# Scores taken relative to key 0 of each head, and key 0's score made from the row maximum, in a cross-attention kernel

## What is computed

```python
def xattn(q, latent_kv, Wq, Wkv_expand, Wout):   # q: 8 x 1024 x 1024, latent_kv: 8 x 64 x 256
    qp = q @ Wq.T
    k, v = split(latent_kv @ Wkv_expand.T, 2)    # 64 keys a batch, 16 heads of 64
    scores = einsum('bhqd,bhkd->bhqk', qh, kh) / sqrt(64)
    scores = where(tril(ones(1024, 64)), scores, finfo.min)
    attn = softmax(scores)
    return (attn @ vh) @ Wout.T

x = x + xattn(layernorm(x), ctx_512, Wq, Wkv_expand, Wout)
x = x + ffn(layernorm(x), weight)                # one fp8-quantised 1024 x 1024 linear layer
```

## Time and profile before

| | us |
|---|---|
| median of 3 runs | 1786.26 (1785.97 to 1786.73) |
| the profiled execution | 1787.1 |
| its span, from first to last instruction | 1785.3 |
| TensorE busy in the span | 1730.4 |
| VectorE busy | 1327.3 |
| ScalarE busy | 688.7 |
| mean granted TensorE clock | 0.988 |

### The profile page before, as it was taken

How to read it: one execution, slowest core, us unless ns; L and a number is a source line. 1 busy time by engine, 2 the same in 40 slices (tenths; PEclk the granted TensorE clock), 3 DMA queues, 4 the chain that set the end, 5 groups by cost and what they waited for, 6 DMA issues and landing times.

```text
span 1785.3 us, 25886 instructions
## 1 busy us (share of the span) xinstructions
PE 1730.4 (97%) x10457; PEld 827.7 (46%) x10482; DVE 1327.3 (74%) x1813; ACT 688.7 (39%) x643; POOL 185.4 (10%) x143
## 2 busy tenths in 40 slices
PE   8689999999999999999999999999999999799998
PEld 4434454445444544454445444544454444344444
DVE  6776778677866787778787878787878665777775
ACT  6632133223322332233223322332233221599996
POOL 0000000000000000000000000000000002155555
PEclk9799999999999999999999999999999999899999
DMA  9674555544555445554555445544553444799995
GB/s 318 155 193 119 126 116 117 131 123 119 111 138 124 110 113 133 133 109 108 132 137 114 107 127 129 129 106 120 136 124 98 119 118 101 250 318 319 319 318 181
DMA packets 404429, 272.15 MB, mean 152 GB/s; under 512 B 355056, under 2 KB 357616, under 8 KB 403824
## 3 DMA queue, kind: packets, MB, share of 16 engines
q1 hardware_dynamic: 404336, 270.84, 57.3%
HBM read 119.28 MB, written 71.30 MB: 107 GB/s over the span
## 4 chain that ended last, share of the span: by engine, by line
PE 91%; issue 5%; DVE 2%; ACT 1%; DMA 1%; POOL 0%; SPq 0%; POOLq 0%; DVEq 0%; ACTq 0%
PE ps_all L636 71%; PE ps_all L772 12%; PE ps_all L623 2%; PE ps_all L609 1%; PE ps_all L610 1%; PE ps_all L645 1%; PE ps_all L706 1%; PE ps_all L588 1%; DVE n_buf L1093 1%; ACT tile_space L869 0%; ACT n_buf L857 0%; DMA tile_space<-tile_space 0%; DVE amax L1072 0%; DMA tile_space<-in_ctx_dram 0%; PE ps_all L578 0%
## 5 line engine op out<-in xcount | busy, mean ns | idle before, releaser
L636 PE MATMUL ps_all<-m_buf,tile_space 128*128 128x512 f16 x3072 | 681.0, 381 | 4.8 <-DVE wo_t L1294 4.8
L636 PE MATMUL ps_all<-n_buf,tile_space 128*128 128x512 f16 x3024 | 670.1, 379 | 0.0
L636 PEld LDWEIGHTS ps_all<-m_buf,tile_space 128*128 128x128 f16 x3072 | 298.0, 98 | 368.8 <-issue 12.2
L636 PEld LDWEIGHTS ps_all<-n_buf,tile_space 128*128 128x128 f16 x3024 | 291.6, 98 | 350.6 <-issue 6.2
L883 ACT ACTIVATE tile_space<-tile_space,neg_mean 128x1024 f32<-128x1024 f32 x63 | 72.4, 1150 | 327.7 <-DVE neg_mean L1180 327.7
L527 POOL TENSOR_TENSOR rstd_x<-veps_x,minus_half 128x1 f32<-128x1 f32 x64 | 35.3, 551 | 1388.4 <-DVE veps_x L1123 1388.4
L879 ACT ACTIVATE tile_space<-tile_space,score_scale 128x1024 f32<-128x1024 f32 x64 | 73.4, 1147 | 230.6 <-DVE tile_space L1150 230.6
L875 ACT ACTIVATE tile_space<-tile_space 128x1024 f16<-128x1024 f32 x64 | 67.6, 1057 | 184.4 <-DVE tile_space L1160 184.4
L1110 DVE SCALAR_TENSOR_TENSOR tile_space<-tile_space 128x1024 f16<-128x1024 f32 x64 | 78.4, 1225 | 64.0 <-ACT tile_space L875 64.0
L772 PE MATMUL ps_all<-wo_t,tile_space 128*128 128x512 bf16 x512 | 119.9, 383 | 2.4 <-DVE tile_space L1401 1.2
L1154 DVE TENSOR_REDUCE hsum<-tile_space 128x16 f32<-128x1024 f32 x64 | 77.9, 1217 | 59.5 <-ACT tile_space L879 59.5
(11 more groups left out here) (131 smaller groups left out, 1700.7 us busy)
## 6 DMA issues: line engine op xcount, KB each, us to landing
tile_space<-in_x_dram SPq DMA_DIRECT2D x128, 512.0 KB, 3.9
x_scratch<-tile_space SPq DMA_DIRECT2D x64, 512.0 KB, 3.0
m_buf<-x_scratch SPq DMA_DIRECT2D x32, 512.0 KB, 5.6
tile_space<-x_scratch SPq DMA_DIRECT2D x32, 512.0 KB, 5.8
out_dram<-m_buf SPq DMA_DIRECT2D x32, 512.0 KB, 4.5
out_dram<-tile_space SPq DMA_DIRECT2D x31, 512.0 KB, 5.0
m_buf<-in_L_xattn_Wq_dram SPq DMA_DIRECT2D x4, 1024.0 KB, 11.1
n_buf<-in_L_xattn_Wout_dram SPq DMA_DIRECT2D x2, 2048.0 KB, 18.3
```

The lines of the kernel that those rows point to most:

```text
L636: mm = nc.tensor.matmul(to[:, cols], left[:, ls, c * P:(c + 1) * P], right[:, rs, c, cols], start=(c == 0 and i == 0), stop=(c == CT - 1 a ...
```

## The change

The scores of each head are taken relative to the score of the head's key 0, which leaves the softmax as it is. So keys are made from the context minus its batch's row 0 (`ctx_d`, one VectorE subtraction during setup, on which TensorE's first `expand` waits), and the column of key 0, which would be zero, is left out of M. M has 63 columns a head: 8 x 63 = 504 of them, contiguous, for each half of the score product. Its `take_m` read 1008 of the 1024 PSUM columns. The score matmuls stream 504 columns, the second half starting 504 columns (1008 bytes) into the block. `make_m` still makes all 64 columns.

Key 0's score in the softmax is made from the maximum of the 63: the row maximum is max(hmax, 0), so key 0's entry is min(-hmax, 0), and this same number is added to the other 63. That is one more small VectorE instruction, with a wait before and after. The maximum and the addition read 2 x 8 x 63 columns. The mask is added in two instructions, one a bank.

```diff
--- before.py
+++ after.py
@@ -64,6 +64,8 @@
     T = B * TB
     KEYS = B * SK
     HALF = 512
+    REST = SK - 1
+    RH = NH // 2 * REST
     assert SK == HD and NP == CT and KEYS == HALF and TB == 8
 
     x_rows = x.rearrange("b s h -> (b s) h")
@@ -162,7 +164,7 @@
         wkv_f = tile_space[:, 8:12, :].rearrange("p a (b l) -> p (a b) l", l=L)
         ctx_f = tile_space[:, 12, :].rearrange("p (a l) -> p a l", l=L)
         wkv_t = tile_space[:, 4:8, :].rearrange("p (a q) r -> p a (q r)", a=LT)
-        ctx_t = tile_space[:, 3, :].rearrange("p (a k) -> p a k", a=LT)
+        ctx_t, ctx_d = (tile_space[:, i, :].rearrange("p (a k) -> p a k", a=LT) for i in (3, 2))
         k_f = wo_t[:, 1].rearrange("p j c -> p (j c)").bitcast(F32).rearrange("p (j k) -> p j k", k=KEYS)
         v_f = w8_raw[:].rearrange("p j c -> p (j c)").bitcast(F32).rearrange("p (j k) -> p j k", k=KEYS)
         k_hi_t, k_lo_t = (tile_space[:, i:i + 2, :].rearrange("p a c -> p (a c)").bitcast(F16)
@@ -185,6 +187,8 @@
         got_wout = [sem(f"got_wout{i}") for i in range(2)]
         turned = sem("turned")
         turned_read = sem("turned_read")
+        ctx_made = sem("ctx_made")
+        key0_made = sem("key0_made")
         wt_full = sem("wt_full")
         wt_hi = sem("wt_hi")
         wt_free = sem("wt_free")
@@ -327,6 +331,18 @@
         KEYS_AT_S = {3: 0, 6: 1}
         KEYS_AT_O = {1: (2,), 2: (3,), 4: (4,), 6: (5,), 7: (6,), 8: (7,)}
 
+        def rest_of(to):
+            return to.rearrange("p (h k) -> p h k", k=SK)[:, :, 1:SK]
+
+        def keys_of(s, c):
+            return m_buf[:, s, c, 0:NH * REST].rearrange("p (h k) -> p h k", k=REST)
+
+        def by_bank(t):
+            return t.rearrange("p (b n) -> p b n", b=2)
+
+        rest_scores = by_bank(ps_s)[:, :, 0:RH].rearrange("p b (h k) -> p b h k", k=REST)
+        sub_heads = sub.rearrange("p (b h k) -> p b h k", b=2, k=SK)
+
         block = scope.enter_context(nc.Block())
 
 
@@ -581,12 +597,15 @@
 
             def expand(g2):
 
+                if g2 == 0:
+                    pe.wait_ge(ctx_made, 1)
+                of = ctx_d if g2 < QUAD else ctx_t
                 to = next_slot()
                 for half in range(2):
                     g = 2 * g2 + half
                     for lt in range(LT):
                         mm = nc.tensor.matmul(to[:, half * HALF:(half + 1) * HALF],
-                                              wkv_t[:, lt, g * P:(g + 1) * P], ctx_t[:, lt, :],
+                                              wkv_t[:, lt, g * P:(g + 1) * P], of[:, lt, :],
                                               start=(lt == 0), stop=(lt == LT - 1))
                 mm.then_inc(turned, 1)
 
@@ -626,6 +645,20 @@
                                 if i == len(PASSES) - 1 and half == 1 and q == 1:
                                     mm.then_inc(grow_full[k], 1)
 
+
+            def scores(left, weave=lambda c: None, ready=lambda c: None):
+                for c in range(CT):
+                    ready(c)
+                    for i, (ls, rs) in enumerate(PASSES):
+                        for half in range(2):
+                            mm = nc.tensor.matmul(ps_s[:, half * HALF:half * HALF + RH],
+                                                  left[:, ls, c * P:(c + 1) * P],
+                                                  m_buf[:, rs, c, half * RH:(half + 1) * RH],
+                                                  start=(c == 0 and i == 0),
+                                                  stop=(c == CT - 1 and i == len(PASSES) - 1))
+                    if c == CT - 1:
+                        mm.then_inc(s_full, 1)
+                    weave(c + 1)
 
             def split_product(to, left, right, full, weave=lambda c: None, ready=lambda c: None):
                 for c in range(CT):
@@ -684,7 +717,7 @@
                             pe.wait_ge(grow_free[c % 2], uses(b + 1, 0, c) + 1)
 
                     between(0)
-                    split_product(ps_s, xt_buf[1 - e], m_buf, s_full, between, m_chunk)
+                    scores(xt_buf[1 - e], between, m_chunk)
                 if last and 1 <= tt <= 4:
                     turn_w8(tt - 1)
                 if b == 2 and is_step(tt, 5):
@@ -746,7 +779,7 @@
             for k in range(2):
                 pe.wait_ge(grow_free[k], QUAD)
             pe.wait_ge(x_turned, 16)
-            split_product(ps_s, xt_buf[0], m_buf, s_full)
+            scores(xt_buf[0])
 
             for b in range(B):
                 batch(pe, b, step, unroll=(b == B - 1))
@@ -859,7 +892,7 @@
 
             def take_m(c, n):
                 act.wait_ge(grow_full[c % 2], n + 1)
-                nc.scalar.activation(m_buf[:, 0, c, :], grow_ps[c % 2][:], ACT.Copy,
+                nc.scalar.activation(keys_of(0, c), rest_of(grow_ps[c % 2][:]), ACT.Copy,
                                      scale=M_SCALE).then_inc(grow_hi[c % 2], 1)
 
             def x_high(t, e):
@@ -1051,6 +1084,11 @@
                 dve.wait_ge(scales_made, n)
 
 
+            dve.wait_ge(turned_read, 1)
+            by_batch = lambda t: t.rearrange("p a (b k) -> p (a b) k", k=SK)
+            nc.vector.tensor_tensor(by_batch(ctx_d), by_batch(ctx_t),
+                                    by_batch(ctx_t)[:, :, 0:1].to_broadcast([P, LT * B, SK]),
+                                    ALU.subtract).then_inc(ctx_made, 1)
             for i in range(4):
                 dve.wait_ge(got_wq[i], 16)
                 nc.vector.tensor_reduce(small[:, 4 + i:5 + i], wq_f[:, 2 * i:2 * i + 2, :], AX.XY, ALU.max,
@@ -1096,8 +1134,8 @@
 
             def take_m(c, n):
                 dve.wait_ge(grow_hi[c % 2], n + 1)
-                nc.vector.scalar_tensor_tensor(out=m_buf[:, 1, c, :], in0=grow_ps[c % 2][:], scalar=M_SCALE,
-                                               in1=m_buf[:, 0, c, :], op0=ALU.mult,
+                nc.vector.scalar_tensor_tensor(out=keys_of(1, c), in0=rest_of(grow_ps[c % 2][:]), scalar=M_SCALE,
+                                               in1=keys_of(0, c), op0=ALU.mult,
                                                op1=ALU.subtract).then_inc(grow_free[c % 2], 1)
 
             def x_low(t, e):
@@ -1137,17 +1175,25 @@
             def mask_scores(t):
 
                 dve.wait_ge(s_full, t + 1)
-                nc.vector.tensor_tensor(heads(ps_s[:]), heads(ps_s[:]),
-                                        causal[:].unsqueeze(1).to_broadcast([P, NH, SK]), ALU.add).then_inc(masked, 1)
+                for half in range(2):
+                    bank = rest_scores[:, half]
+                    mm = nc.vector.tensor_tensor(bank, bank, causal[:, 1:SK].unsqueeze(1).to_broadcast([P, NH // 2, REST]),
+                                                 ALU.add)
+                mm.then_inc(masked, 1)
 
             def maxima(t, masks=None):
                 if masks is None:
                     dve.wait_ge(s_full, t + 1)
                 else:
                     dve.wait_ge(masked, masks)
-                nc.vector.tensor_reduce(hmax[:], heads(ps_s[:]), AX.X, ALU.max).then_inc(max_done, 1)
+                nc.vector.tensor_reduce(by_bank(hmax[:]), rest_scores, AX.X, ALU.max).then_inc(max_done, 1)
                 dve.wait_ge(max_done, t + 1)
-                nc.vector.tensor_tensor(heads(sub), heads(ps_s[:]), across(hmax[:]), ALU.subtract).then_inc(s_read, 1)
+                nc.vector.tensor_scalar(sub_heads[:, :, :, 0], by_bank(hmax[:]), -1.0, 0.0, ALU.mult,
+                                        ALU.min).then_inc(key0_made, 1)
+                dve.wait_ge(key0_made, t + 1)
+                nc.vector.tensor_tensor(sub_heads[:, :, :, 1:SK], rest_scores,
+                                        sub_heads[:, :, :, 0:1].to_broadcast([P, 2, NH // 2, REST]),
+                                        ALU.add).then_inc(s_read, 1)
 
             def sums(t):
                 dve.wait_ge(exp_done, t + 1)
```

## The result

| | before, us | after, us |
|---|---|---|
| median (5 runs each) | 1786.26 (1785.42 to 1786.8) | 1778.16 (1777.52 to 1778.99) |
| the profiled execution | 1787.1 | 1777.52 |
| its span | 1785.3 | 1775.7 |
| TensorE / VectorE / ScalarE busy | 1730.4 / 1327.3 / 688.7 | 1720.3 / 1337.6 / 687.3 |
| mean granted TensorE clock | 0.988 | 0.988 |

The ratio of the times is 0.9953, with a 95% interval of 0.9942 to 0.9965: faster by 8.1 us, or 0.5%. The forecast was 1777.0, so the time is 1.2 us above it, inside the stated range.

A forecast was written before the change was run, and what follows sets the result against it. During the attention, the columns TensorE streams were taken to set the time. -9.92 - 0.20 + 0.42 + 0.22 + 0.17 = -9.31 us took the profiled 1787.1 to 1777.8, less 0.84 a median of 1777.0 us; own range 1775.2 to 1779.8.

The forecast's parts named there:

- The pace of 504 columns: Score matmuls on TensorE: 212.5 ns each, 3.33 ns less than at 512 columns; 9.92 us over tiles 2 to 63.
- Tile 0's wait: TensorE's wait for N's read-out before tile 0's last N pair: 0.06 us longer in batches 1 to 7, 0.42 us.
- The batch: The period of a batch, seven times: shorter by 8 x 0.16 - 0.06 = 1.22 us.
- VectorE's chain: From score product to read scores in every tile: small instruction +0.20, shorter reads -0.03, so +0.17 us, hidden in usual tiles.
- The mask pair: Once a batch on VectorE, two mask instructions of 504 columns for one of 1024: +0.05 us.
- The covers: Slack elsewhere, cost 0: tile 6 uses 0.17 of 0.8 us, tile 7 0.38 of 0.60, setup's subtraction has 1.9.
- The ends: First tile: mask and chain +0.22 us, shorter score product -0.20; last tile's output product waits +0.17 us.
- The sum: All terms together: -9.92 - 0.20 + 0.42 + 0.22 + 0.17 = -9.31 us, for a median of 1777.0 us.
- rival (b) in its first form: Weight loads set part of the score matmuls' pace; only a third of 9.92 us comes through: 1784.2 us, 3%.
- with 0.5 for the small instruction: VectorE's small instruction at 0.5 instead of 0.20 us: about 0.1 us a batch, 0.6 at the ends, +1.3.
- rival (c): VectorE slow on runs of 63 columns; tile 6 waits 3.0 us in each of 7 batches: 1798 us, 3%.

The follow-up runs named there:

- e2_512: Changed kernel with the score matmuls streaming 512 columns again, all the rest of the change kept: 1786.51 us, ratio 1.0000 to the kernel before.
- e3_496: Changed kernel with 62 keys a head, 496 columns a score matmul, key 1 also left out: 1767.84 us, ratio 0.9898 to the kernel before.
- e5_order: Changed kernel with ScalarE's read-out of the sixth N block moved before x_high in tile 0 of a batch: 1773.11 us, ratio 0.9927.
- e1_same: Changed kernel, unedited, timed again beside the kernel before: 1778.55 us, ratio 0.9952.
- e4_offset: Changed kernel with the second half starting 1024 bytes into a block of M, not 1008, widths unchanged: 1777.67 us, ratio 0.9952.
- e7_more6: Changed kernel with six more small dependent VectorE instructions after the maximum in every tile: 1807.99 us, ratio 1.0123 to the kernel before.

## Why the prediction came out right, step by step

- **The pace of 504 columns.** Forecast 212.5 ns, measured 212.5; e2_512 and e3_496 show it from both sides. The slope through 64, 128 and 512 columns was the right price. The Trainium skill's page "TensorE: Matmul & The Clock Gate", section "Back-to-back issue gap", gives 81 and 131 ns at 128 and 512 columns for pairs of load and matmul, and that doesn't hold here: the 128-column transposes take 56 ns, 512 take 215.8 and 496 take 209.2.
- **Tile 0's wait.** Forecast 0.06 us more for each batch, measured 0.06, and again 0.06 for eight columns more. Cause and size are shown by e5_order: the wait goes when x_high is moved.
- **The batch.** Forecast 1.22 us less, measured 1.22 in all seven.
- **VectorE's chain.** The small instruction was put at 0.20 us and takes 0.184, with a step of 0.21 to the next; the chain grew by 0.18 to 0.19, forecast 0.17. The mask pair grew by 0.04 (forecast 0.05).
- **The covers.** Tile 7 keeps 0.23 us (0.60 - 0.38 = 0.22), tile 6 0.63 (0.80 - 0.17 = 0.63), setup 1.2. `expand` starts at 10.89 (11.25 before), so the subtraction delays nothing.
- **The ends.** The last output product waits 0.14 us longer (forecast 0.17), and 0.33 longer in e1_same. The output product of tile 0 starts 0.42 us earlier, at 117.86; the forecast of +0.22 - 0.20 us for the first tiles had put no gain there. In e1_same it starts at 117.18, in e2_512, which streams as many columns as the kernel before, at 117.63. These differences between executions are as large as the terms or larger, so the terms are not confirmed.
- **The sum.** The profiled executions differ by 1787.1 - 1777.5 = 9.6 us, forecast 9.3. Of these 8.53 lie in the seven batches and 0.42 before them. Then 0.83 lie in the last batch, six score products at 0.16 less the longer wait, and what follows took 0.19 more. The medians differ by 8.1, and by 7.9 in e1_same, so they fall short of the forecast by over 1 us. The forecast took 0.84 us off its figure because the profiled execution of the kernel before was that much above its median; the profiled execution of the changed kernel was 0.64 us below its own. So the agreement of 1777.5 with the forecast's 1777.8 is in part luck. What is missing is of the size of one stretch at the lower clock level (1.6 us), and two profiles of the same kernel differ by just such a stretch. That explains a difference of this size; it isn't shown that the change makes the stretch more frequent. There is little room for a lasting loss: e4_offset, which has the same batch period, gained 8.8 us, and 496 columns gained 18.6, 9.3 for each eight columns. The prediction's own range had allowed for the difference.
- **The prediction's figures.** Its lower bound of 1775.2 is 0.3 us under its own working (1777.0 - 1.5 = 1775.5). The time of rival (b) in its first form is 0.8 too high: 3.3 less 0.4 us of gain leave a median of 1783.4, while 1784.2 is the same gain taken from the profiled execution. Neither changes a chance or the forecast.

**The step that was wrong** didn't decide: "with 0.5 for the small instruction [...] tiles 6 and 7 still hold, tile 7 just not: about 0.1 us a batch [...] so +1.3". Two more instructions (0.61 us in all, a little beyond that bound) were expected to cost 0.9 us by the same working, and cost 3.1 to 3.5: tile 6 did not hold in four of the seven batches, which is 2.0 of it. What exactly 0.5 would cost was not run. The prediction read tile 6 in batch 1 alone, where VectorE has no quantisation beside it and comes 0.30 us early with two more as well, and it looked at the idle time of the tile itself, not at whether VectorE enters it on time. The same gap is in rival (c): its 21 us were worked out from one cover, while e7_more6, with 1.28 us more, lost 29 us against the changed kernel. For tile 7 the 0.1 us a batch was not seen either: with two more, batches 1 and 2 keep their period.

What stays open: why the median gained about 1 us less than the sum; why the clock level at 117 us falls in one execution and not in another; whether the small instruction can be had for less (a form of it without its own waits wasn't tried).

## To carry to other kernels

Where TensorE streams without a gap, as here, a saving is worth its number of columns times the slope, and the rest of the sum is a list of places where another engine has to be in time; price each by its slack, and re-read it in every kind of batch, since spare time that an engine needs over several tiles isn't seen in one tile. A wait that the change lengthens is worth a look of its own: here moving one ScalarE instruction behind another gave 5 us, over half of what the change itself gave. Before a loop of short matmuls is trimmed, time the widths: here 63 columns gained nothing over 64, and 48 gained 4.0 ns of the 6.7 that the line gives.

## What was not expected of the hardware

- 63 columns cost as much as 64 (29.1 ns), and a moving operand that starts 2 bytes off costs 29.9; at 504 columns a start at 1008 bytes costs nothing.
- Matmuls of 48 columns follow each other at 25.1 ns, not at the 22.5 of the line.
- Going from 128-row matmuls to 64-row ones costs about 0.09 us, with no wait.
- The stretch from 117.0 to 120.4 us at the lower clock level, behind a wait of 2 us that in another execution left the clock as it was, moves the time by 1.6 us: more than the difference between several of the kernels here.
